# Sums of squares of queries and keys on column groups of TensorE, in plain 32-bit precision

## The chip, the cores and the metric

The kernel runs on one core of a Trainium2 chip. The metric is the device time of one execution in microseconds; of the kernel before there are three runs. All engines of the core have their own instruction stream and are kept in step by semaphores: TensorE (PE, its weight loads PEld), VectorE (DVE), ScalarE (ACT), GpSimd (POOL) and SyncE (SP), which issues the loads.

## The reference

A layer in two steps on 1024 tokens of width 256. The first is cross attention over 16 sequences of 64 tokens, 16 heads of 128, in which queries and keys are normed per head; the second is causal self attention with 16 heads and a routed gated network. Here the first matters:

```python
def rmsnorm(x, g, eps=1e-5):
    var = jnp.mean(jnp.square(x), axis=-1, keepdims=True)
    return x * jax.lax.rsqrt(var + eps) * g
q = rmsnorm((hidden_states @ Wq).reshape(B, Sq, H, D), gq)
k = rmsnorm((encoder_hidden_states @ Wk).reshape(B, Skv, H, D), gk)
scores = jnp.einsum('bqhd,bkhd->bhqk', q, k) * scale
attn = jax.nn.softmax(scores, axis=-1)
out = jnp.einsum('bhqk,bkhd->bqhd', attn, v)
return out.reshape(B, Sq, H * D) @ Wo
```

So each query and each key needs the sum of squares over its 128 channels.

## The kernel before

The tokens are cut in two halves of 512 (HT), each four tiles of 128 (NT). The stages run in the order a (cross attention) half 0 and 1, b (self attention) half 0 and 1, m (gated network) half 0 and 1. A unit of stages a and b is one head (16 a half), a unit of stage m one chunk of 128 hidden channels (25 a half). Each engine's stream is written out by hand: a function `head(u)` per engine issues, for unit u, the scores and softmax of u together with the projections of the next unit (`nxt`) and the weight splits of the one after (`after`). Beside some units stand pieces of other work (`prepare`): the norming and turning of the tokens of a later stage, named in `plan_of`. The units between run in a hardware loop of two.

Most products are made in the 32-bit form that TensorE streams at full rate (float32r) from operands that are split into a high and a low part, with three matmuls in place of one; plain float32 operands are used for the small products, and such a matmul shows as two in the trace.

In stage a, for head u, TensorE's `head` (L629) issues: the scores of u (`scores`, L567, eight 128x64 by 128x64 float32 products on alternate halves of the array's columns, so 16 instructions); the attention-value product of the head before (`attn_values`, L587); the keys and queries of the next head (`project_keys`, `project_first`, L426, three and six matmuls of 512 columns); the output product of the head before into two accumulators (`output`, L468, twelve of 256 columns); in half 0 a product of two weights (`value_out`, L533); the sums of squares of the next head's keys (`norm_k`, L553); the turn of the attention (`turn_attn`, L575); the sums of squares of the next head's queries (`norm_q`, L540).

The sums before. Queries: ScalarE writes sq_q (float32) from bank_q, and `norm_q` multiplies each tile of it, as the stationary operand, with a column of ones, one column of bank_v a tile. Keys: ScalarE squares bank_k twice, into sq_k (float32, L768) and sq_k_hi (float32r, L769), GpSimd writes the rest sq_k_lo (L1211 is the line of all its subtractions), and `norm_k` adds both with a stationary `ones_of` that puts the even sequence of a tile on partitions 0 to 63 and the odd one on 64 to 127, four matmuls of 256 columns. Then ScalarE takes the logarithm of both (`log_k` L792, `log_q` L788), GpSimd adds them (`add_logs`, L1255), ScalarE makes the inverse root (`roots`, L798), and VectorE scales the scores with it (L1025).

VectorE's `head` (L1136) after the softmax (attention written in two halves, L1043) copies the next queries (`take_q`, L1050), writes the high parts of the weights of the head after the next (`split_first` L1061, `split_second` L1073), and in half 0 the low part of the weight product (L1159). GpSimd's `head` (L1258) issues the square split, then the low parts of those weights, then `add_logs`.

Of the kernel before, what the change touches and what calls it, by code (L numbers as in the profile page):

```python
# [32 lines left out]
P = 128  # L33
# [118 lines left out]
def flamingo_layer(nc, x, ctx_t, ctx, head_a, head_b, pair_v, chunk_m, small, out, shared_units):  # L152
# [5 lines left out]
    SETUP = 8  # L158
# [28 lines left out]
    with ExitStack() as stack:  # L187
# [22 lines left out]
        ones, ones_of = sb("ones", [P, 1]), sb("ones_of", [P, SPB, P], F32R)  # L210
# [24 lines left out]
        sq_k_hi, sq_k_lo = sb("sq_k_hi", [P, HT], F32R), sb("sq_k_lo", [P, HT], F32R)  # L235
# [48 lines left out]
        A = stage_sems("a", "wq_hi wq_lo wk_hi wk_lo q_done k_done sq_q sq_k sq_k_hi sq_k_lo qt kt scores scaled max "  # L284
# [134 lines left out]
        def _(pe):  # L419
# [116 lines left out]
            def norm_q(u):  # L536

                pe.wait_ge(A["sq_q"], u.done())
                for t in range(NT):
                    last = nc.tensor.matmul(bank_v[:, D + t:D + t + 1], sq_q[:, t * P:(t + 1) * P], ones[:],  # L540
                                            start=True, stop=True)
                last.then_inc(A["ssq_done"], 1)

            def norm_k(u):

                pe.wait_ge(A["sq_k_lo"], u.done())
                if not u.very_first:
                    pe.wait_ge(A["scaled"], u.done(1))
                for s in range(SPB):
                    for part, square in enumerate((sq_k_hi, sq_k_lo)):  # L550
                        keys = square[:].rearrange("p (t s k) -> p t s k", s=SPB, k=SEQ)[:, :, s, :]
                        first, final = s + part == 0, s + part == SPB
                        last = nc.tensor.matmul(bank_s[:, NT * SEQ:2 * NT * SEQ], ones_of[:, s, :], keys,  # L553
                                                start=first, stop=final)
                last.then_inc(A["ssk_done"], 1)
# [73 lines left out]
            def head(u):  # L629
                prev, nxt = u.prev(), u.next()  # L630

                scores(u)
                if prev and prev.deferred:
                    attn_values(prev)
                if nxt.kind == "a":
                    project_keys(nxt)
                project_first(nxt)
                second_tiles = u.kind == "b" and not u.odd
                if second_tiles:
                    project_values(u, True)  # L640
                if u.kind == "a":
                    pe.wait_ge(A["ln_q"], u.done())
                if prev:
                    pe.wait_ge(stages[prev.kind]["pv_lo"], prev.done())
                held = prepare(u)
                if prev:
                    output(prev)
                if nxt.kind == "b" and not second_tiles:
                    project_keys(nxt)
                values_of_a = u.kind == "a" and u.half == 0  # L650
                if values_of_a and not held:
                    value_out(u)
                if nxt.kind == "a":
                    norm_k(nxt)
                turn_attn(u)
                if nxt.kind == "b" and second_tiles:
                    project_keys(nxt)
                for semaphore, value in held:
                    pe.wait_ge(semaphore, value)
                if values_of_a and held:  # L660
                    value_out(u)
                if nxt.kind == "a":
                    norm_q(nxt)
                if nxt.kind == "b" and not second_tiles:
                    project_values(nxt, False)
                if not u.deferred:
                    attn_values(u)
                if u.first:
                    clear_acc(u)
# [26 lines left out]
            norm_k(start)  # L696
            for kind, half in STAGES:
                run_units(pe, kind, half, chunk if kind == "m" else head)
# [3 lines left out]
        def _(act_e):  # L702
# [63 lines left out]
            def square_k(u):  # L766
                act_e.wait_ge(A["k_done"], u.done())
                nc.scalar.activation(sq_k[:], bank_k[:], ACT.Square, scale=SCALE).then_inc(A["sq_k"], 1)  # L768
                nc.scalar.activation(sq_k_hi[:], bank_k[:], ACT.Square, scale=SCALE).then_inc(A["sq_k_hi"], 1)  # L769
# [15 lines left out]
            def log_q(u):  # L785

                act_e.wait_ge(A["ssq_done"], u.done())
                nc.scalar.activation(ln_q[:], bank_v[:, D:D + NT], ACT.Ln, bias=eps5[:, 0:1]).then_inc(A["ln_q"], 1)  # L788
# [123 lines left out]
        def _(v):  # L912
# [141 lines left out]

            def split_first(u, user):
# [80 lines left out]
            def head(u):  # L1136
# [6 lines left out]
                take_q(nxt)  # L1143
                split_first(after, u)
# [55 lines left out]
            take_q(start)  # L1200
            split_first(start.next(), None)
# [6 lines left out]
        def _(pool):  # L1208
# [38 lines left out]
            def split_squares(u):  # L1247
                if u.kind == "a":
                    pool.wait_ge(A["sq_k_hi"], u.done())
                    rest(sq_k_lo[:], sq_k[:], sq_k_hi[:], A["sq_k_lo"])  # L1250

# [6 lines left out]
            def head(u):  # L1258
                nxt = u.next()
                after = nxt.next()  # L1260
                split_squares(nxt)
# [25 lines left out]
            nc.gpsimd.memset(ones_of[:].bitcast(F32), 0.0).then_inc(setup_pool, 1)  # L1287
            pool.wait_ge(setup_pool, SETUP - SPB)
            for s in range(SPB):
                nc.gpsimd.memset(ones_of[:, s, s * SEQ:(s + 1) * SEQ].bitcast(F32), 1.0).then_inc(setup_pool, 1)  # L1290
# [9 lines left out]
            split_squares(start)  # L1300
# [75 lines left out]
```

## Time and profile before

| what | value |
|---|---|
| runs | 749.43, 747.45, 749.66 us (median 749.43) |
| profiled execution, span from the first to the last instruction | 746.0 us |
| profiled execution, its own time around the span | not shown on the page |
| mean granted TensorE clock | 0.995 |
| busy: TensorE, weight loads | 724.7 us (97%), 640.1 us (86%) |
| busy: VectorE, ScalarE, GpSimd | 512.8 (69%), 370.9 (50%), 316.0 us (42%) |
| HBM | 49.3 MB by the load queue, 66 GB/s |

Times are in microseconds from the first instruction, means in nanoseconds. "Busy" of TensorE is the union of records whose ends are modelled and overlap the next start, so a share of 97% does not say that it streams all the time; the distance between the starts of matmuls says how fast it goes. A row of the timeline merges equal instructions that follow one another: its duration reaches from the first start to the last end. "Idle before" names the instruction of another engine that ended the wait.

### The profile page before, as it was taken

The numbers are of one execution on the slowest core, as the hardware profiler recorded it, in microseconds if no ns is written. First come the engines' busy times: TensorE is split into PE (matmuls) and PEld (weight loads), VectorE is DVE, ScalarE is ACT, GpSimd is POOL, SyncE is SP. The second block draws the span as 40 slices with busy tenths as digits, with TensorE's granted clock in tenths as the row PEclk, the third lists the DMA queues.
The fourth block names the chain that finished last, engine by engine and source line by source line (L and its number), as shares of the span: only waits on it lengthen the run. The fifth ranks groups of instructions, "written<-read, shape, count | busy, mean of one in ns | idle before, by whom it ended". The sixth has DMA issues, their size and how long they took to land.

```text
span 746.0 us, 15617 instructions
## 1 busy us (share of the span) xinstructions
PE 724.7 (97%) x5370; PEld 640.1 (86%) x5370; DVE 512.8 (69%) x1129; ACT 370.9 (50%) x776; POOL 316.0 (42%) x404
## 2 busy tenths in 40 slices
PE   7999999999998899999999999999999999999997
PEld 5899998888897789998888998888888888888886
DVE  4576768756576776778786787887655688655555
ACT  3667776657667533333443443334444754444442
POOL 3434343433443424333434333442555466555553
PEclk9999999999999999999999999999999999999999
DMA  8112121000100011221211221121233332333332
GB/s 277 43 44 63 42 64 54 22 25 29 32 22 22 7 45 58 86 62 58 78 57 58 89 61 57 58 65 36 70 100 85 85 85 85 88 102 85 94 95 85
DMA packets 36588, 49.88 MB, mean 67 GB/s; under 512 B 3904, under 2 KB 23744, under 8 KB 36544
## 3 DMA queue, kind: packets, MB, share of 16 engines
q1 hardware_dynamic: 36544, 49.29, 22.6%
q8 instruction: 28, 0.46, 0.3%
q14 instruction: 16, 0.13, 0.1%
HBM read 48.22 MB, written 1.05 MB: 66 GB/s over the span
## 4 chain that ended last, share of the span: by engine, by line
PE 66%; DVE 19%; ACT 5%; issue 4%; POOL 3%; DMA 2%; SPq 1%; DVEq 0%; POOLq 0%
PE acc L468 15%; PE bank_q L426 11%; PE bank_k L426 10%; PE bank_p L587 6%; PE bank_v L525 5%; PE bank_s L426 4%; PE bank_v L426 4%; PE bank_s L567 4%; PE bank_t L575 2%; PE bank_v L540 2%; DMA raw_b<-in_head_b 2%; DVE attn L1043 2%; DVE pv_lo L1015 1%; DVE qt L1050 1%; DVE sc_sub L1034 1%
## 5 line engine op out<-in xcount | busy, mean ns | idle before, releaser
L468 PE MATMUL acc<-wo_hi,pv_hi 128*128 128x256 f32 x328 | 93.4, 285 | 2.0 <-DVE pv_lo L1112 1.4
L468 PE MATMUL acc<-wo_hi,pv_lo 128*128 128x256 f32 x328 | 92.6, 282 | 0.0
L468 PE MATMUL acc<-wo_lo,pv_hi 128*128 128x256 f32 x328 | 92.0, 280 | 0.0
L1211 POOL TENSOR_TENSOR wq_lo<-raw_b,wq_hi 128x256 fp32r<-128x256 f32 x32 | 24.1, 753 | 152.3 <-DVE wq_hi L1064 152.3
L1211 POOL TENSOR_TENSOR sq_k_lo<-sq_k,sq_k_hi 128x512 fp32r<-128x512 f32 x32 | 41.2, 1288 | 79.0 <-ACT sq_k_hi L769 79.0
L426 PE MATMUL bank_q<-xt_hi,wq_hi 128*128 128x512 f32 x178 | 73.9, 415 | 0.0
L1211 POOL TENSOR_TENSOR wq_lo<-raw_m,wq_hi 128x256 fp32r<-128x256 f32 x50 | 43.4, 869 | 67.0 <-DVE wq_hi L1067 67.0
L426 PE MATMUL bank_q<-xt_hi,wq_lo 128*128 128x512 f32 x178 | 70.5, 396 | 0.0
L426 PE MATMUL bank_q<-xt_lo,wq_hi 128*128 128x512 f32 x178 | 70.5, 396 | 0.0
L1015 DVE TENSOR_TENSOR pv_lo<-bank_p,pv_hi 128x512 fp32r<-128x512 f32 x64 | 43.9, 686 | 35.8 <-ACT pv_hi L803 35.8
L468 PEld LDWEIGHTS acc<-wo_hi,pv_hi 128*128 128x128 f32 x328 | 61.7, 188 | 6.9 <-DVE pv_lo L1112 2.2
L468 PEld LDWEIGHTS acc<-wo_lo,pv_hi 128*128 128x128 f32 x328 | 61.7, 188 | 2.6
L824 ACT ACTIVATE ex<-sc_sub 128x256 f32<-128x256 f32 x64 | 26.8, 418 | 70.7 <-DVE sc_sub L1034 69.4
L468 PEld LDWEIGHTS acc<-wo_hi,pv_lo 128*128 128x128 f32 x328 | 61.8, 188 | 0.0
L815 ACT ACTIVATE pv_hi<-hh 128x512 fp32r<-128x512 f32 x50 | 31.6, 632 | 59.5 <-DVE hh L1108 59.5
L1043 DVE TENSOR_TENSOR attn<-ex,ex_inv 64x256 f32<-64x256 f32 x128 | 57.4, 448 | 4.2
L1112 DVE TENSOR_TENSOR pv_lo<-hh,pv_hi 128x512 fp32r<-128x512 f32 x50 | 36.7, 734 | 34.2 <-ACT pv_hi L815 34.2
L1101 DVE TENSOR_TENSOR gu<-gs,unit_w 128x512 f32<-128x512 f32 x44 | 32.3, 734 | 37.6 <-ACT gs L809 37.3
L803 ACT ACTIVATE pv_hi<-bank_p 128x512 fp32r<-128x512 f32 x64 | 38.2, 597 | 39.2 <-PE bank_p L587 39.1
L1211 POOL TENSOR_TENSOR wk_lo<-raw_m,wk_hi 128x256 fp32r<-128x256 f32 x50 | 40.6, 811 | 37.7 <-ACT wk_hi L869 37.7
L1211 POOL TENSOR_TENSOR wq_lo<-raw_a,wq_hi 128x256 fp32r<-128x256 f32 x32 | 23.3, 727 | 68.9 <-DVE wq_hi L1061 68.9
L1037 DVE TENSOR_REDUCE ex_sum<-ex 128x4 f32<-128x256 f32 x64 | 26.9, 420 | 31.5 <-ACT ex L824 31.5
(192 smaller groups left out, 2166.4 us busy)
## 6 DMA issues: line engine op xcount, KB each, us to landing
raw_m<-in_chunk_m SPq DMA_DIRECT2D x50, 256.0 KB, 2.7
raw_a<-in_head_a SPq DMA_DIRECT2D x48, 192.0 KB, 2.4
raw_b<-in_head_b SPq DMA_DIRECT2D x32, 256.0 KB, 2.8
raw_m<-in_chunk_m SPq DMA_DIRECT2D x50, 128.0 KB, 2.0
raw_v<-in_pair_v SPq DMA_DIRECT2D x16, 256.0 KB, 2.6
raw_b<-in_head_b SPq DMA_DIRECT2D x32, 128.0 KB, 2.0
xs<-in_x SPq DMA_DIRECT2D x8, 128.0 KB, 3.7
out<-xs SPq DMA_DIRECT2D x4, 256.0 KB, 2.3
```

Source lines behind the costliest of these rows:

```text
L426: last = nc.tensor.matmul(bank[:], w[:, cols], m(k), start=n == 0, stop=n == 3 * chunks - 1)
L468: last = nc.tensor.matmul(acc[t // 2][:, (t % 2) * D:(t % 2 + 1) * D], w[:, tok], m, start=False, stop=True, skip_group_check=True)
L525: last = nc.tensor.matmul(bank_v[:, b * PAIR:(b + 1) * PAIR], m, w[:, cols], start=n == 0, stop=n == 3 * KD - 1)
L567: last = nc.tensor.matmul(bank_s[s * SEQ:(s + 1) * SEQ, t * SEQ:(t + 1) * SEQ], qt[:, tok], kt[:, tok], start=True, stop=True)
L587: last = nc.tensor.matmul(bank_p[:, t * P:(t + 1) * P], value, attn_t[:, t * P:(t + 1) * P], start=True, stop=True)
L803: nc.scalar.activation(pv_hi[u.parity][:], bank_p[:], ACT.Copy).then_inc(stage["pv_hi"], 1)
L815: nc.scalar.activation(pv_hi[u.parity][:], hh[:], ACT.Copy).then_inc(M["hh_hi"], 1)
L1015: nc.vector.tensor_tensor(pv_lo[u.parity][:], bank_p[:], pv_hi[u.parity][:], ALU.subtract).then_inc(stage["pv_lo"], 1)
L1043: nc.vector.tensor_tensor(attn[rows, :, s * SEQ:(s + 1) * SEQ], ex[rows], ex_inv[rows].unsqueeze(2).to_broadcast([SEQ, NT, SEQ]), ALU.mult)\
L1101: nc.vector.tensor_tensor(gu[:], gs[:], weights, ALU.mult).then_inc(M["weighted"], 1)
L1112: nc.vector.tensor_tensor(pv_lo[u.parity][:], hh[:], pv_hi[u.parity][:], ALU.subtract).then_inc(M["hh_lo"], 1)
L1211: nc.gpsimd.tensor_tensor(lo, raw, hi, ALU.subtract).then_inc(signal, 1)
```

## The change

The query sums turn the operands round: a 128x32 piece of ones is stationary and sq_q streams, tile t going to partitions 32t to 32t+31 of bank_p. VectorE copies that 128x128 block (`take_rows`), TensorE transposes it into bank_q (`turn_q`), and ScalarE reads its sums from there. The key sums take sq_k alone, in float32, with 64 columns of ones stationary, one matmul for each half of the partitions. sq_k_hi, sq_k_lo and GpSimd's square split go. `norm_q` moves up to right behind `output` (where a piece is held, behind that), and the wait for the logarithm of the query sums moves up ahead of `project_first`, which overwrites bank_q.

```diff
--- before.py
+++ after.py
@@ -155,7 +155,8 @@
     C = ctx.shape[1]
     CH = chunk_m.shape[0]
     E = 16
-    SETUP = 8
+    SETUP = 6
+    GROUP = 32
     TOP = 6
     WARM_UP = 20
     HT = TOK // HALVES
@@ -207,7 +208,7 @@
         xt_hi = [sb(f"xt_hi{h}", [P, KD, HT], F32R) for h in range(HALVES)]
         xt_lo = [sb(f"xt_lo{h}", [P, KD, HT], F32R) for h in range(HALVES)]
         hn = sb("hn", [P, NT, D])
-        ones, ones_of = sb("ones", [P, 1]), sb("ones_of", [P, SPB, P], F32R)
+        ones, ones_w = sb("ones", [P, 1]), sb("ones_w", [P, SEQ])
         zeros = sb("zeros", [P, 512], F32R)
         eps5, eps6 = sb("eps5", [P, 1]), sb("eps6", [P, 1])
         tg = sb("tg", [P, 2])
@@ -232,7 +233,7 @@
         vo_hi, vo_lo = sb("vo_hi", [P, H, D], F32R), sb("vo_lo", [P, H, D], F32R)
 
         sq_q, sq_k = sb("sq_q", [P, HT]), sb("sq_k", [P, HT])
-        sq_k_hi, sq_k_lo = sb("sq_k_hi", [P, HT], F32R), sb("sq_k_lo", [P, HT], F32R)
+        rows_q = sb("rows_q", [P, P])
         qt, kt = sb("qt", [P, HT]), sb("kt", [P, HT])
         vs = sb("vs", [P, NT, PAIR])
         ln_k, ln_q = sb("ln_k", [P, NT, SEQ]), sb("ln_q", [P, NT])
@@ -281,7 +282,7 @@
 
             return {n: sem(f"{tag}_{n}") for n in names.split()}
 
-        A = stage_sems("a", "wq_hi wq_lo wk_hi wk_lo q_done k_done sq_q sq_k sq_k_hi sq_k_lo qt kt scores scaled max "
+        A = stage_sems("a", "wq_hi wq_lo wk_hi wk_lo q_done k_done sq_q sq_k rows_done rows qt kt scores scaled max "
                        "sub exp sum inv norm_lo norm_hi t_done attn_t vo_done vo_hi vo_lo ssk_done ssq_done ln_q "
                        "ln_k ln_qk r_qk pv_done pv_hi pv_lo wo_done")
 
@@ -537,21 +538,25 @@
 
                 pe.wait_ge(A["sq_q"], u.done())
                 for t in range(NT):
-                    last = nc.tensor.matmul(bank_v[:, D + t:D + t + 1], sq_q[:, t * P:(t + 1) * P], ones[:],
+                    rows = slice(t * GROUP, (t + 1) * GROUP)
+                    last = nc.tensor.matmul(bank_p[rows, 0:P], ones_w[:, 0:GROUP], sq_q[:, t * P:(t + 1) * P],
                                             start=True, stop=True)
-                last.then_inc(A["ssq_done"], 1)
+                last.then_inc(A["rows_done"], 1)
+
+            def turn_q(u):
+
+                pe.wait_ge(A["rows"], u.done())
+                nc.tensor.transpose(bank_q[:, 0:P], rows_q[:], ident).then_inc(A["ssq_done"], 1)
 
             def norm_k(u):
 
-                pe.wait_ge(A["sq_k_lo"], u.done())
+                pe.wait_ge(A["sq_k"], u.done())
                 if not u.very_first:
                     pe.wait_ge(A["scaled"], u.done(1))
                 for s in range(SPB):
-                    for part, square in enumerate((sq_k_hi, sq_k_lo)):
-                        keys = square[:].rearrange("p (t s k) -> p t s k", s=SPB, k=SEQ)[:, :, s, :]
-                        first, final = s + part == 0, s + part == SPB
-                        last = nc.tensor.matmul(bank_s[:, NT * SEQ:2 * NT * SEQ], ones_of[:, s, :], keys,
-                                                start=first, stop=final)
+                    keys = sq_k[:].rearrange("p (t s k) -> p t s k", s=SPB, k=SEQ)[:, :, s, :]
+                    last = nc.tensor.matmul(bank_s[s * SEQ:(s + 1) * SEQ, NT * SEQ:2 * NT * SEQ], ones_w[:], keys,
+                                            start=True, stop=True)
                 last.then_inc(A["ssk_done"], 1)
 
             def scores(u):
@@ -634,17 +639,19 @@
                     attn_values(prev)
                 if nxt.kind == "a":
                     project_keys(nxt)
+                if u.kind == "a":
+                    pe.wait_ge(A["ln_q"], u.done())
                 project_first(nxt)
                 second_tiles = u.kind == "b" and not u.odd
                 if second_tiles:
                     project_values(u, True)
-                if u.kind == "a":
-                    pe.wait_ge(A["ln_q"], u.done())
                 if prev:
                     pe.wait_ge(stages[prev.kind]["pv_lo"], prev.done())
                 held = prepare(u)
                 if prev:
                     output(prev)
+                if nxt.kind == "a" and not held:
+                    norm_q(nxt)
                 if nxt.kind == "b" and not second_tiles:
                     project_keys(nxt)
                 values_of_a = u.kind == "a" and u.half == 0
@@ -659,8 +666,10 @@
                     pe.wait_ge(semaphore, value)
                 if values_of_a and held:
                     value_out(u)
+                if nxt.kind == "a" and held:
+                    norm_q(nxt)
                 if nxt.kind == "a":
-                    norm_q(nxt)
+                    turn_q(nxt)
                 if nxt.kind == "b" and not second_tiles:
                     project_values(nxt, False)
                 if not u.deferred:
@@ -694,6 +703,7 @@
             project_first(start)
             norm_q(start)
             norm_k(start)
+            turn_q(start)
             for kind, half in STAGES:
                 run_units(pe, kind, half, chunk if kind == "m" else head)
 
@@ -766,7 +776,6 @@
             def square_k(u):
                 act_e.wait_ge(A["k_done"], u.done())
                 nc.scalar.activation(sq_k[:], bank_k[:], ACT.Square, scale=SCALE).then_inc(A["sq_k"], 1)
-                nc.scalar.activation(sq_k_hi[:], bank_k[:], ACT.Square, scale=SCALE).then_inc(A["sq_k_hi"], 1)
 
             def take_k(u):
                 if u.kind == "a":
@@ -785,7 +794,8 @@
             def log_q(u):
 
                 act_e.wait_ge(A["ssq_done"], u.done())
-                nc.scalar.activation(ln_q[:], bank_v[:, D:D + NT], ACT.Ln, bias=eps5[:, 0:1]).then_inc(A["ln_q"], 1)
+                sums = bank_q[:, 0:P].rearrange("p (t c) -> p t c", c=GROUP)[:, :, 0]
+                nc.scalar.activation(ln_q[:], sums, ACT.Ln, bias=eps5[:, 0:1]).then_inc(A["ln_q"], 1)
 
             def log_k(u):
                 act_e.wait_ge(A["ssk_done"], u.done())
@@ -1052,6 +1062,11 @@
                     v.wait_ge(B["q_done"], u.done())
                     nc.vector.tensor_copy(qt[:], bank_q[:]).then_inc(B["qt"], 1)
 
+            def take_rows(u):
+
+                v.wait_ge(A["rows_done"], u.done())
+                nc.vector.tensor_copy(rows_q[:], bank_p[:, 0:P]).then_inc(A["rows"], 1)
+
             def split_first(u, user):
 
                 if user:
@@ -1141,6 +1156,8 @@
                 if turning:
                     prepare_piece(*piece_at(u), u)
                 take_q(nxt)
+                if nxt.kind == "a":
+                    take_rows(nxt)
                 split_first(after, u)
                 if after.kind != "m":
                     split_second(after, u)
@@ -1198,6 +1215,7 @@
             prepare_piece("norm", ("x", 0))
             prepare_piece("turn", ("x", 0))
             take_q(start)
+            take_rows(start)
             split_first(start.next(), None)
             split_second(start.next(), None)
             for kind, half in STAGES:
@@ -1244,11 +1262,6 @@
                     pool.wait_ge(M["wd_hi"], u.done())
                     rest(wo_lo[u.parity][:], raw_m2[u.parity][:], wo_hi[u.parity][:], M["wd_lo"])
 
-            def split_squares(u):
-                if u.kind == "a":
-                    pool.wait_ge(A["sq_k_hi"], u.done())
-                    rest(sq_k_lo[:], sq_k[:], sq_k_hi[:], A["sq_k_lo"])
-
             def add_logs(u):
                 pool.wait_ge(A["ln_k"], u.done())
                 pool.wait_ge(A["ln_q"], u.done())
@@ -1258,7 +1271,6 @@
             def head(u):
                 nxt = u.next()
                 after = nxt.next()
-                split_squares(nxt)
                 split_first(after)
                 split_second(after)
                 if nxt.kind == "a":
@@ -1284,10 +1296,7 @@
             nc.gpsimd.memset(attn[:], 0.0).then_inc(setup_pool, 1)
             nc.gpsimd.memset(eps5[:], 1e-5).then_inc(setup_pool, 1)
             nc.gpsimd.memset(eps6[:], 1e-6).then_inc(setup_pool, 1)
-            nc.gpsimd.memset(ones_of[:].bitcast(F32), 0.0).then_inc(setup_pool, 1)
-            pool.wait_ge(setup_pool, SETUP - SPB)
-            for s in range(SPB):
-                nc.gpsimd.memset(ones_of[:, s, s * SEQ:(s + 1) * SEQ].bitcast(F32), 1.0).then_inc(setup_pool, 1)
+            nc.gpsimd.memset(ones_w[:], 1.0).then_inc(setup_pool, 1)
             def split_context(half):
                 pool.wait_ge(ctxt_hi_ready, half + 1)
                 toks = slice(half * HT, (half + 1) * HT)
@@ -1297,7 +1306,6 @@
             split_first(start)
             split_second(start)
             split_context(0)
-            split_squares(start)
             split_first(start.next())
             split_second(start.next())
             add_logs(start)
```

## Rows read from the trace of the kernel before

**Rows 1.** Page, part 1: busy us (share of the span) xinstructions.

```profile
PE 724.7 (97%) x5370; PEld 640.1 (86%) x5370; DVE 512.8 (69%) x1129; ACT 370.9 (50%) x776; POOL 316.0 (42%) x404
```

**Rows 2.** Timeline, a head of half 0: start us, us, engine line op out<-in xcount.

```profile
62.24 0.59 PE L533 MATMUL bank_v<-raw_a 128*128 128x256 f32 x2
...
63.03 0.28 PE L553 MATMUL bank_s<-sq_k_lo,ones_of 128*128 128x256 f32 x1
...
63.16 0.60 PE L575 MATMUL bank_t<-sm,attn 128*128 128x128 f32 x4
...
63.35 0.47 ACT L792 ACTIVATE ln_k<-bank_s,eps 128x256 f32<-128x256 f32 x1 [1.15 <-PE bank_s L553]
...
63.59 0.95 PE L540 MATMUL bank_v<-ones,sq_q 128*128 128x1 f32 x8
...
63.79 0.60 ACT L840 ACTIVATE attn_t<-bank_t 128x512 f32<-128x512 f32 x1
...
64.47 0.69 PE L567 MATMUL bank_s<-kt,qt 128*64 128x64 f32 x16
...
65.08 1.16 PE L587 MATMUL bank_p<-attn_t,ctx_sb 128*128 128x128 f32 x8
...
68.18 0.28 PE L468 MATMUL acc<-vo_hi,pv_hi 128*128 x1
...
69.60 0.59 PE L533 MATMUL bank_v<-raw_a 128*128 128x256 f32 x2
...
71.83 0.69 PE L567 MATMUL bank_s<-kt,qt 128*64 128x64 f32 x16
```

**Rows 3.** Timeline of TensorE, a head of half 1.

```profile
165.47 0.69 PE L567 MATMUL bank_s<-kt,qt 128*64 128x64 f32 x16
...
170.98 0.28 PE L553 MATMUL bank_s<-sq_k_lo,ones_of 128*128 128x256 f32 x1
171.25 0.66 PE L575 MATMUL bank_t<-sm,attn 128*128 128x128 f32 x4
...
172.63 0.28 PE L567 MATMUL bank_s<-kt,qt 128*64 128x64 f32 x2
```

**Rows 4.** Timeline of VectorE and GpSimd, the same head of half 1.

```profile
164.07 0.69 DVE L1050 COPY qt<-bank_q 128x512 f32<-128x512 f32 x1
164.80 0.29 DVE L1061 CAST wq_hi<-raw_a 128x256 fp32r<-128x256 f32 x1
...
165.17 0.73 POOL L1211 TENSOR_TENSOR wq_lo<-raw_a,wq_hi 128x256 fp32r<-128x256 f32 x1 [1.87 <-DVE wq_hi L1061]
...
166.27 0.61 POOL L1255 TENSOR_TENSOR ln_qk<-ln_k,ln_q 128x256 f32<-128x256 f32 x1
...
167.37 0.42 DVE L1025 TENSOR_TENSOR sc<-bank_s,r_qk 128x256 f32<-128x256 f32 x1 [2.14 <-ACT r_qk L798]
...
171.23 0.69 DVE L1050 COPY qt<-bank_q 128x512 f32<-128x512 f32 x1
```

**Rows 5.** Groups: attention of 30:120 us, then of 157:215; squares of the whole span.

```profile
L1043 DVE TENSOR_TENSOR attn<-ex,ex_inv 64x256 f32<-64x256 f32 x24 | 12.6, 524 | 0.8
...
L1043 DVE TENSOR_TENSOR attn<-ex,ex_inv 64x256 f32<-64x256 f32 x16 | 6.7, 420 | 0.5
...
L1211 POOL TENSOR_TENSOR sq_k_lo<-sq_k,sq_k_hi 128x512 fp32r<-128x512 f32 x32 | 41.2, 1288 | 79.0 <-ACT sq_k_hi L769 79.0
```

**Rows 6.** Group of the smallest cast of VectorE, 30:225 us.

```profile
L1073 DVE CAST wk_hi<-raw_a 128x128 fp32r<-128x128 f32 x26 | 5.7, 220 | 0.0
```

**Rows 7.** Timeline of TensorE in narrow windows around the scores of 64.47.

```profile
64.29 0.25 PE L540 MATMUL bank_v<-ones,sq_q 128*128 128x1 f32 x1
...
64.75 0.40 PE L567 MATMUL bank_s<-kt,qt 128*64 128x64 f32 x8
65.08 0.49 PE L587 MATMUL bank_p<-attn_t,ctx_sb 128*128 128x128 f32 x2
```

**Rows 8.** Tile bank_s: engine op xcount: duration ns min/median/max, first and last start, forms.

```profile
L567 PE MATMUL bank_s<-kt,qt x1024: 221/222/369, 19.8 to 517.2; 128*64 128x64 f32 x171
```

## The prediction

> **What bounds the kernel now.** The times first: three runs, median 749.43 us. The page's first part says that TensorE holds a matmul record 97% of the span [rows 1]; the ends of these records are modelled, so I read the distance between starts instead. All edits lie in stage a (32 heads out of 64, then 50 chunks), so I cut one steady head out of each half of that stage.
>
> Half 0 [rows 2]: the score matmuls (L567) start at 64.47 and again at 71.83, one head in 7.36 us. In between nothing on TensorE has a hole: twelve output matmuls of 256 columns take 69.60 - 68.18 = 1.42, 0.118 each; the value product (L533) starts at 62.24; the last of the four sums of key squares (L553) at 63.03, so it ends its slot at 63.15 and the four took 4 x 0.12 = 0.48, which leaves 62.67 - 62.24 = 0.43 for L533; the turn of the attention (L575) follows at 63.16, the query sums (L540) at 63.59, the scores at 64.47. L575 stands right at the end of the slot before it, so what it reads wasn't late. TensorE binds this half.
>
> Half 1 has no L533, so its TensorE work is 7.36 - 0.43 = 6.93. Its head takes 172.63 - 165.47 = 7.16 [rows 3]: TensorE waits, 170.98 + 0.12 = 171.10 to 171.25 in front of L575, for the attention. What makes the attention late is a ring over four engines [rows 4]: VectorE copies qt at 164.07, as soon as it has written the attention; then wq_hi at 164.80, GpSimd wq_lo at 165.17, wk_lo, the sum of logarithms at 166.27, ScalarE's root, VectorE's scaling at 167.37, the softmax, and the next qt at 171.23. From qt to qt 7.16, and each link starts when the one before it ends. So two loops matter: TensorE's list (7.36 and 6.93) and the ring. In half 0 the ring also closes in 7.36, since there the two attention products take 524 ns on average against 420 in half 1 [rows 5], 0.21 for the pair, while GpSimd's square split overlaps them. Without that it is 7.15.
>
> **The ring after.** It gains one link: take_rows stands on VectorE between qt and wq_hi. No 128x128 copy out of PSUM is in the trace. Lower bound: the 128x128 cast, 0.22 [rows 6]; upper bound: qt, four times the columns, with its distance to the next instruction, 164.80 - 164.07 = 0.73. The 128x256 read of PSUM (L1025, 0.42) and the 128x512 one (0.69) [rows 4] give (0.69 - 0.42)/256 = 1.05 ns a column, so 128 columns are 0.69 - 384 x 0.00105 = 0.29; I take 0.30. Its wait for rows_done is no cost, because norm_q now runs right behind the output product. What the edit takes from the ring is only the overlap with the square split: 0.21 in half 0, nothing in half 1. sq_k_hi on ScalarE (one instruction a head) and the split on GpSimd (32 x 1.29) [rows 5] lie beside TensorE work otherwise; their removal I cost at nothing, and at most at a gain of 0.2 a head, if ScalarE's exponential stands behind sq_k_hi on the ring. The ring becomes 7.15 + 0.30 = 7.45 in both halves. Bounds of the link 0.22 and 0.73: 7.37 to 7.88.
>
> **TensorE's list after.** Removed: the four L553 (0.48) and the eight L540. Those reach from 63.59 to 64.29 + 0.11 = 64.40 [rows 2, 7], 0.81. Together 1.29. Added: eight passes of 128 columns with a 32-wide stationary, four passes of 256 columns with a 64-wide one, and one transpose (a quarter of L575's 0.43: 0.11). The scores are the only matmuls on column groups in the trace, and they show both sides of the trade. Gain: the last eight start within 0.40 less the 0.22 of one record, 0.18, so 0.026 apart [rows 7, 8], where half of a 128-column pass (L587: eight take 1.16 - 0.28 = 0.88 from first to last start, 0.21 of it the first step, so 0.67/6 = 0.112 each) would be 0.056; two groups run at once. Cost: from the end of L540, 64.40, to the first score 0.07, and the start is slow by 0.04 (0.69 - 0.22 = 0.47 from first to last start, against 15 steps of 0.028, 0.43); at the far end the last score has ended its slot at 64.93 + 0.06 = 64.99, the next full-width matmul starts at 65.08, and from it to its follower are 0.49 - 0.28 = 0.21 instead of 0.11 [rows 7]. One excursion into column groups and back costs 0.11 + 0.20 = 0.31.
> Query sums: with two groups at once 8 x 0.112 / 2 = 0.45, plus 0.31 = 0.76. Key sums: a 256-column pass is 0.216 (half of L533), 4 x 0.216 / 2 = 0.43, plus 0.31 = 0.74. With the transpose 1.61 added, 1.29 removed: +0.32 a head. List: 7.68 in half 0, 7.25 in half 1. Bounds: four groups at once and no excursion cost, 0.22 + 0.43 + 0.11 = 0.76, i.e. -0.53; nothing at once and both excursions, 1.21 + 1.17 + 0.11 = 2.49, i.e. +1.20. I take the middle since it is the row of the scores, the nearest.
> In the trace the way out of column mode costs about 0.2 us [rows 7]. The Trainium skill says why (TensorEngine Tiling (Array Packing), Key Properties): changing the tiling mode drains the engine. By that rule the change adds two such changes back and forth where one was, and the trace agrees. Against it stands a rule of the page TensorE: Matmul & The Clock Gate (Part 3): column tiles overlap nearly fully, span about one matmul plus 4 ns a tile. By it the query sums would stream 0.23 instead of 0.45, an estimate from that page; half 0 would then be bound by the ring.
>
> **Waits that the edits add.** (a) PE waits for ln_q before project_first, since bank_q now holds the turned sums. Behind it are six projections. ln_q would end about 1.5 us after the scores start, project_first comes 2.3 after (its six matmuls of 0.233 end at 68.18): no cost, 0.3 at worst. (b) turn_q waits for rows: attention end + qt 0.72 + rows 0.32 = 1.05 behind it, and turn_q stands 0.43 behind the start of L575. Where the ring binds, TensorE idles there but nothing is added: the period is the larger of the two loops. (c) Scores wait for ln_k (0.47 [rows 2]); before, 0.88 of query sums lay between L575 and the scores, now 0.11. ln_k ends about 0.5 behind the start of L575, scores come at 0.61: no wait. But attn_t follows in ScalarE's queue (ends 64.39, where L587 starts at 65.08 [rows 2]): it would now end 1.3 behind the start of L575, where L587 wants to start at 1.23: 0.07 in half 0, hidden in half 1. I leave it in the range. (d) In the two heads whose unit turns tokens (one in each half), norm_q stands behind the turn: norm_q, rows and turn_q follow one another with nothing between, 0.3 more each, 0.6.
>
> **The sum.** Half 0: the larger of 7.45 and 7.68 against 7.36: +0.32, 15 heads, 4.8. Half 1: the larger of 7.45 and 7.25 against 7.15: +0.30, 16 heads, 4.8. Heads with a VectorE piece beside them are longer but hang on VectorE, so the copy costs them the same. Plus (d) 0.6. Prologue: two memsets fewer on GpSimd come out in the warm-up matmuls, and the first scores wait for ln_k as before: 0. Stages b and m have no edit. In all +10.2 us on the profiled execution's span of 746.0, i.e. 756.2. The page gives no time for it around the span; the median of the runs lies 3.4 above the span, and with that left as it is: 759.6; I say 759.5.
>
> **Rivals.** (1) Passes run in the order of issue: the two passes of one group can't overlap, so only neighbours do: query sums five steps of 0.112 + 0.31 = 0.87, key sums three of 0.216 + 0.31 = 0.96; list +0.65: half 0 8.01 + 0.07, half 1 7.58. 15 x 0.72 + 16 x 0.43 + 0.6 = 18: 768. For it: both passes of a score share a group. Against: the scores start in even pairs. (2) No overlap at all for these shapes: +1.20: half 0 8.56, half 1 8.13: 15 x 1.2 + 16 x 0.98 + 0.6 = 34: 784. The scores speak against it. (3) The excursions cost nothing here and four groups run at once; then only the ring binds, with the copy at 0.22: half 0 7.37, half 1 +0.22: 4 us, 753; if the ring has 0.2 of play that I don't see, it is no change, 750. (4) Faster: TensorE's list binds both halves and the ring gives way, because what GpSimd and ScalarE drop shortens it by more than the copy adds. The place is L575, the price the list's -0.53 in 15 heads of half 0: -8, 741. It decides once streams and excursions together are below the 1.29 removed and the ring below 7.36. Against it: half 1 lost 0.43 of TensorE work and gained only 0.20.
>
> **Chances.** My forecast 0.57 (its own range 756 to 763), rival 1 0.18, rival 2 0.05, rival 3 0.14 (half of it within no change), rival 4 0.06. A difference under 0.3%, 2.2 us, can't be told from none. Faster 0.06, same 0.07, slower 0.87. Range 752.5 to 769.
>
> **What would show it.** Right: the head of half 1 at about 7.45, with wq_hi 1.03 behind qt instead of 0.73, and TensorE idle before turn_q; the head of half 0 at about 7.7 with no TensorE hole; 0.1 to 0.2 at each change of column mode; the attention product at 420 ns in half 0. Wrong: a rows copy far from 0.29, starts of the new sums that are not 0.06 (queries) and 0.11 (keys) apart on average, or a wait for ln_k before the scores.

## The result: slower by 0.53%, less than half of the forecast

| kernel | median us | runs | ratio to before, 95% interval |
|---|---|---|---|
| before | 747.48 | 8 | |
| changed | 751.95 | 8 | 1.0053 [1.0034, 1.0072] |

The change costs 4.5 us. The forecast was +10.2 us, 759.5, range 752.5 to 769: the right side, less than half of the size, and 0.55 us below the range. Of the 7.5 us between 759.5 and 751.95, 2 lie in the base: the forecast stood on the 749.43 of three runs, where eight give 747.48. The other 5.6 are the change's own price.

Two words of the prediction come back below. TensorE's list is what TensorE has to work through in one head, one piece behind the other. The ring is the loop over VectorE, GpSimd and ScalarE that makes the attention of a head; a link is one instruction of it. The longer of the two sets the time of a head.

The changed kernel's page, part 1 (answers to [rows 1]): GpSimd is busy for 41 us less and ScalarE for 21, TensorE for 2.8 more.

```profile
PE 727.5 (97%) x5402; PEld 608.9 (81%) x5402; DVE 515.1 (68%) x1161; ACT 349.7 (46%) x744; POOL 274.7 (37%) x370
```

**Half 0**, the timeline of the changed kernel, one head (answers to [rows 2]):

```profile
64.28 0.28 PE L469 MATMUL acc<-vo_hi,pv_lo 128*128 x1
64.49 0.43 PE L542 MATMUL bank_p<-sq_q,ones_w 128*32 128x128 f32 x8
64.84 0.70 PE L534 MATMUL bank_v<-raw_a 128*128 128x256 f32 x2
65.47 0.65 PE L558 MATMUL bank_s<-sq_k,ones_w 128*64 128x256 f32 x4
66.06 0.66 PE L580 MATMUL bank_t<-sm,attn 128*128 128x128 f32 x4
66.17 0.47 ACT L802 ACTIVATE ln_k<-bank_s,eps 128x256 f32<-128x256 f32 x1 [1.66 <-PE bank_s L558]
66.55 0.27 PE L549 MATMUL bank_q<-sm,rows_q 128*128 128x128 f32 x1
66.79 0.69 PE L572 MATMUL bank_s<-kt,qt 128*64 128x64 f32 x16
...
74.34 0.69 PE L572 MATMUL bank_s<-kt,qt 128*64 128x64 f32 x16
```

Scores to scores 7.55, before 7.36. The eight query passes take 0.43 from the first start to the last end; one record is about 0.27 long, so all eight start within 0.16, and with the 0.11 of the last pass they stream for 0.27. Two passes of one group take 0.22 alone (0.11 each, as in the attention's turn): the four groups run at once. The output ends its slot at 64.40 and the weight product works from 64.94 (its second pass starts 0.32 behind its first instead of 0.22, so I count the 0.10 to the way out, as in [rows 7]): the query sums cost 0.55, where I had 0.76. From the end of the weight product at 65.37 to the turn of the attention (0.05 after its first start, which waits for its load) are 0.74: the key sums as forecast. Where the 0.10 and the 0.05 belong is my choice; the sum of both, 1.29, is not. The transpose is 0.11.

**Half 1**, the ring (answers to [rows 4]), timeline of VectorE and GpSimd:

```profile
182.81 0.69 DVE L1060 COPY qt<-bank_q 128x512 f32<-128x512 f32 x1
...
183.42 0.28 DVE L1068 COPY rows_q<-bank_p 128x128 f32<-128x128 f32 x1
183.73 0.29 DVE L1076 CAST wq_hi<-raw_a 128x256 fp32r<-128x256 f32 x1
...
184.10 0.72 POOL L1229 TENSOR_TENSOR wq_lo<-raw_a,wq_hi 128x256 fp32r<-128x256 f32 x1 [5.64 <-DVE wq_hi L1076]
...
190.16 0.69 DVE L1060 COPY qt<-bank_q 128x512 f32<-128x512 f32 x1
```

qt to qt 7.35, before 7.16, and even from head to head; the scores of these heads come alternately 7.03 and 7.67 apart (7.35 on average), so below a half 1 is told by its mean. The row copy lasts 0.28, as worked out, but starts 0.08 before the end of qt: from qt to wq_hi are 0.92 where 0.73 were, so the link is worth 0.19, not 0.30.

**Where VectorE was slowed.** The groups of the attention products, 30:120 us (answers to [rows 5]), then the subtraction of the maximum in the head that turns tokens, in the kernel before with the GpSimd instruction beside it, and in the changed one:

```profile
L1053 DVE TENSOR_TENSOR attn<-ex,ex_inv 64x256 f32<-64x256 f32 x24 | 10.1, 420 | 0.8
```
```profile
127.02 1.27 POOL L1211 TENSOR_TENSOR sq_k_lo<-sq_k,sq_k_hi 128x512 fp32r<-128x512 f32 x1 [2.51 <-ACT sq_k_hi L769]
127.58 0.99 DVE L1034 TENSOR_TENSOR sc_sub<-sc,sc_max 128x256 f32<-128x256 f32 x1
```
```profile
131.36 0.42 DVE L1044 TENSOR_TENSOR sc_sub<-sc,sc_max 128x256 f32<-128x256 f32 x1
```

Beside GpSimd's square split that subtraction took 0.99, without it 0.42, so 0.57 of VectorE's time is gone. The head itself, from scores to scores, fell only from 10.05 to 9.76: the query edit takes part of it again (see the key edit alone, where it is 8.91).

### The profile page after: what moved, and what is told of

It reads as the page before. It is cut to its first block, busy times and chain, and to the rows that moved or that the text cites. A ratio compares the mean times of both kernels' runs of the same rounds, so it can differ in the third digit from the quotient of the medians.

```text
span 752.2 us, 15661 instructions
## 1 busy us (share of the span) xinstructions
PE 727.5 (97%) x5402; PEld 608.9 (81%) x5402; DVE 515.1 (68%) x1161; ACT 349.7 (46%) x744; POOL 274.7 (37%) x370
## 4 chain that ended last, share of the span: by engine, by line
PE 70%; DVE 18%; ACT 4%; issue 3%; POOL 2%; DMA 2%; SPq 1%; DVEq 0%; POOLq 0%
PE acc L469 16%; PE bank_q L427 12%; PE bank_k L427 10%; PE bank_p L592 6%; PE bank_v L526 5%; PE bank_s L427 4%; PE bank_v L427 4%; PE bank_s L572 4%; PE bank_t L580 3%; PE bank_s L558 2%; DVE attn L1053 1%; DVE pv_lo L1025 1%; DMA raw_b<-in_head_b 1%; PE bank_v L534 1%; DVE sc_sub L1044 1%
## 5 line engine op out<-in xcount | busy, mean ns | idle before, releaser
L1053 DVE TENSOR_TENSOR attn<-ex,ex_inv 64x256 f32<-64x256 f32 x128 | 53.8, 420 | 4.2
L850 ACT ACTIVATE attn_t<-bank_t 128x512 f32<-128x512 f32 x64 | 38.2, 597 | 21.1 <-PE bank_t L580 18.0
```

The costliest lines, as they stand in the source:

```text
L850: nc.scalar.activation(attn_t[:], bank_t[:], ACT.Copy).then_inc(stage["attn_t"], 1)
L1053: nc.vector.tensor_tensor(attn[rows, :, s * SEQ:(s + 1) * SEQ], ex[rows], ex_inv[rows].unsqueeze(2).to_broadcast([SEQ, NT, SEQ]), ALU.mult)\
```

## Experiments

All times of heads are distances between first scores. "Steady" is the mean of 13 heads of half 0 and of 9 of half 1; the last four intervals around the end of half 0 and the last five of half 1 hold the heads with a piece beside them. Before: steady 7.36 and 7.15, sums 34.98 and 43.39. Changed: 7.55 and 7.33, 35.00 and 42.82. The expectations weigh theory A (list and ring, with the prices above) against theory B (the query rows and the moved waits are the loss, the key edit is harmless).

**The clock in these sums.** They can't be compared as they stand. In some executions TensorE runs part of one of these heads at 1.2 GHz. The same interval, the fourth of the nine, is 8.39 us before and 7.20 with the key edit alone, and it is 8.06 and 6.90 in two executions of the changed kernel. Its windows (the third number from the end is the granted clock), before, key edit alone, changed in its second profile:

```profile
149.93:158.32 8.39, 8.39 (x62) 7.68 (x62) 4.64 (x11) 4.24 (x8) 1.60 (x2) 0.83 0.08 23
```
```profile
151.57:158.77 7.20, 7.20 (x62) 6.18 (x62) 4.43 (x11) 4.26 (x8) 0.59 (x1) 1.00 0.10 28
```
```profile
151.67:158.57 6.90, 6.90 (x63) 5.53 (x63) 4.62 (x12) 3.37 (x8) 0.09 (x1) 1.00 0.09 29
```

The column probe below, in which the square split and the query sums are those of the kernel before, has 7.14 there at full clock. So 1.25 of the 34.98 before and 1.16 of the 35.00 changed are clock: 33.7 and 33.8 without them.

**Key edit alone.** The diff of the sums, on the kernel before:

```diff
-                    for part, square in enumerate((sq_k_hi, sq_k_lo)):
...
+                    last = nc.tensor.matmul(bank_s[s * SEQ:(s + 1) * SEQ, NT * SEQ:2 * NT * SEQ], ones_w[:], keys,
```

> The kernel before with the key edit alone (float32, two column groups of 64, no second square, no square split on GpSimd); query sums as before. Theory A (two loops with prices): TensorE's list gains 0.735 - 0.48 = +0.25 a head, so half 0 goes from 7.36 to 7.61; the ring gets no link and stays at 7.15, so half 1 is bound by a list of 6.93 + 0.25 = 7.18, about where it was; the heads with a VectorE piece beside them get back up to 0.5 each, because the square split no longer slows VectorE. In all +1 to +3 us. Theory B (the loss comes from the query rows and the moved waits, key edit harmless): no change or a little faster.

Measured 747.7, ratio 0.9996 [0.9982, 1.0011]. No change, where +1 to +3 us was expected. Steady heads 7.62 and 7.19, as expected; the heads with a piece gave back more than I allowed, sums 32.45 and 41.59, that is 2.5 and 1.8 us less than before. 1.25 of the 2.5 is the clock; 3.1 in all is left for the square split, 1.14, 0.95 and 0.95 of it in three of the long heads (10.05 to 8.91, 9.41 to 8.46, 9.73 to 8.78). So the key edit's price in half 0, 3.4, and its gain in the heads with pieces cancel but for the scatter of the runs. One head in the timeline of TensorE, 7.62 from scores to scores:

```profile
65.34 0.69 PE L566 MATMUL bank_s<-kt,qt 128*64 128x64 f32 x16
...
71.00 0.65 PE L552 MATMUL bank_s<-sq_k,ones_w 128*64 128x256 f32 x4
...
72.96 0.51 PE L566 MATMUL bank_s<-kt,qt 128*64 128x64 f32 x10
```

**Query edit alone.** On the changed kernel:

```diff
-                pe.wait_ge(A["sq_k"], u.done())
+                pe.wait_ge(A["sq_k_lo"], u.done())
...
+                split_squares(nxt)
                 split_first(after)
```

> The changed kernel with the key sums of before (split squares, four full-width matmuls). Theory A: the list changes by 0.55 + 0.11 + 0.06 - 0.81 = -0.09, the ring by the row copy, +0.20, and the square split keeps slowing VectorE: half 0 up to 7.5, half 1 7.35, heads with a piece 0.2 longer: +5 to +6 us on before, so slower than the whole change (+4.5) although it holds only half of its edits. Theory B: as the whole change, +4.5. A rival C (column groups for the keys are the loss): near no change.

Measured 751.57, ratio 1.0058 [1.0036, 1.0079]: as much as the whole change, not more. By their totals the two single edits come out as theory B has it; the heads decide against B, since the key edit alone makes each steady head of half 0 0.26 longer. Steady 7.41 and 7.34. So the net loss is the query edit's: the key edit pays for itself. Half 1 is the ring with its link. The heads with a piece, sums 34.10 and 43.74, are some 0.7 above those of before at full clock (33.7 and 43.39) in all. The attention products of half 0 still take 451 ns on average, against 420: 0.06 a head.

**Rows copied later on VectorE.**

```diff
                 take_q(nxt)
-                if nxt.kind == "a":
-                    take_rows(nxt)
                 split_first(after, u)
                 if after.kind != "m":
                     split_second(after, u)
+                if nxt.kind == "a":
+                    take_rows(nxt)
```

> The changed kernel, but VectorE copies the rows after the two weight casts instead of ahead of them, so the copy is off the ring. Theory A: the ring is back at 7.15, the list (7.52 and 7.09) is not: half 0 stays at 7.55, half 1 falls from 7.35 to about 7.15: 2.5 to 3 us faster than the changed kernel, +1.5 to +2 on before. Theory B: turn_q and the scores come later, so no gain, or slower.

Measured 752.05, ratio 1.0057 [1.0035, 1.0080]: no gain. Steady 7.63 and 7.31. My expectation was wrong, since there is a second ring, through TensorE. The timeline of this kernel, half 1:

```profile
170.19 0.69 DVE L1025 TENSOR_TENSOR pv_lo<-bank_p,pv_hi 128x512 fp32r<-128x512 f32 x1 [0.25 <-ACT pv_hi L813]
...
174.33 0.28 DVE L1068 COPY rows_q<-bank_p 128x128 f32<-128x128 f32 x1
...
174.67 0.14 PEld L549 LDWEIGHTS bank_q<-sm,rows_q 128*128 128x128 f32 x1 [0.33 <-DVE rows_q L1068]
...
174.93 0.69 PE L572 MATMUL bank_s<-kt,qt 128*64 128x64 f32 x16
```

TensorE now waits for the rows, the scores and all behind them come later, and so does pv_hi, for which VectorE waits 0.25 in the middle of the softmax in every second head; the copies of qt come alternately 7.20 and 7.51 apart. The copy had only changed rings.

**Rows copied by ScalarE.**

```diff
+            def take_rows(u):
+                act_e.wait_ge(A["rows_done"], u.done())
+                nc.scalar.activation(rows_q[:], bank_p[:, 0:P], ACT.Copy).then_inc(A["rows"], 1)
...
+                if nxt.kind == "a" and not turning:
+                    take_rows(nxt)
                 if nxt.kind == "a":
                     log_k(nxt)
```

> The changed kernel, but ScalarE copies the rows (ahead of the logarithm of the keys), in the place of its dropped second square; turn_q then waits for the copy of the queries too. Theory A: as the late copy on VectorE, half 1 7.15, half 0 at the list, 7.5: +1.5 to +2 us on before, and VectorE is the shorter by 0.28 a head. Theory B: no gain on the changed kernel.

Measured 748.65, ratio 1.0009 [0.9995, 1.0024]: 3.3 us of the 4.5 are gone. Steady 7.55 and 7.12: half 0 is still the list's, half 1 is back at the ring without a link. ScalarE copies beside qt:

```profile
186.67 0.28 ACT L797 ACTIVATE rows_q<-bank_p 128x128 f32<-128x128 f32 x1 [0.53 <-PE bank_p L542]
186.67 0.69 DVE L1071 COPY qt<-bank_q 128x512 f32<-128x512 f32 x1
187.39 0.29 DVE L1082 CAST wq_hi<-raw_a 128x256 fp32r<-128x256 f32 x1
```

**The two sums side by side.**

```diff
-                if nxt.kind == "a" and not held:
-                    norm_q(nxt)
...
                 if values_of_a and not held:
                     value_out(u)
+                if nxt.kind == "a" and not held:
+                    norm_q(nxt)
```

> The changed kernel with the weight product (value_out) ahead of the query sums, so that the query and key sums stand side by side in half 0 as they do in half 1. Theory A (each way into and out of column groups costs time on TensorE's list): from the end of the output product to the turn of the attention half 1 of the changed kernel takes 1.08, half 0 less its weight product 1.28; so half 0 falls by 0.20 a head to 7.35: 3 us faster than the changed kernel. Rival (the modes cost nothing, half 0 is held by a wait): half 0 stays at 7.55.

Measured 750.13, ratio 1.0020 [1.0000, 1.0039], against a before of 748.56 on that chip. Steady 7.36 and 7.31: the 0.19 of half 0, as expected.

**Both moves.**

> Both moves: rows copied by ScalarE, query and key sums side by side. Theory A: list 7.35 in half 0 and 6.9 in half 1, ring 7.15: half 0 at 7.35, half 1 at 7.12: 3 us less than with the copy on ScalarE alone (748.65), 745.6, and so 2 us faster than the kernel before. Rival: no gain from the place of the sums, 748.6.

Measured 746.27, ratio 0.9968 [0.9950, 0.9986], with both diffs above: 0.3% faster than the kernel before. Steady 7.35 and 7.12. This is the version that beats both. Its steady heads are nearly those of the kernel before (0.3 us in all), so they don't explain the gain of 2.4 us. Part of it is the clock: the mean granted clock of its 12 runs is 0.999, of the runs before 0.995, and where the whole run had 1.000 its four runs took 744.2 to 744.9 and the two of before 745.6 and 745.7, about 1.2 less. Whether the edits bring the steadier clock no run shows. The heads with a piece are 1.7 shorter than before at full clock (sums 32.96 and 42.41 against 33.7 and 43.39), but stage b is as much longer (252.4, see below), so where the rest of the gain lies stays open. Timeline of TensorE, half 0, the sums now without a full-width product between them:

```profile
70.31 0.69 PE L573 MATMUL bank_s<-kt,qt 128*64 128x64 f32 x16
75.47 0.59 PE L534 MATMUL bank_v<-raw_a 128*128 128x256 f32 x2
75.99 0.43 PE L542 MATMUL bank_p<-sq_q,ones_w 128*32 128x128 f32 x8
76.35 0.65 PE L559 MATMUL bank_s<-sq_k,ones_w 128*64 128x256 f32 x4
76.93 0.66 PE L581 MATMUL bank_t<-sm,attn 128*128 128x128 f32 x4
77.67 0.53 PE L573 MATMUL bank_s<-kt,qt 128*64 128x64 f32 x11
```

**What the way in and out costs, by itself.** Two probes on the kernel before, one execution each; the second uses `ident` and 128 partitions instead:

```diff
+                nc.tensor.matmul(bank_v[0:32, D + 16:D + 17], ones_w[:, 0:32], ones[:], start=True, stop=True)
```

> The kernel before with one additional float32 matmul of one column ahead of each weight product of half 0, on a column group of 32 (its result is not used). It streams next to nothing, so it prices the way in and out. Theory A: 0.3 a head, half 0 from 7.36 to 7.66. Rival (free): 7.4.

> Control to the probe: the same matmul at full width (stationary 128x128, result not used). Two loads of 0.112 that nothing hides: half 0 at 7.36 + 0.22 = 7.58, with no gap at either end. If the column probe is not above this one less about 0.17 (its loads are a quarter), the way in and out costs nothing.

Half 0 7.71 and 7.58, half 1 as before (7.15). So a 32-wide product of one column costs 0.35, a full-width one 0.22. The full-width loads start 0.11 apart, and two of them that nothing covers are the 0.22; the 32-wide loads start 0.026 apart, so 0.05 of the 0.35 is loads. The way in and out is 0.3. The column probe, then the full one:

```profile
65.53 0.69 PE L571 MATMUL bank_s<-kt,qt 128*64 128x64 f32 x16
70.77 0.22 PE L546 MATMUL bank_v<-ones,ones_w 128*32 128x1 f32 x2
...
73.25 0.69 PE L571 MATMUL bank_s<-kt,qt 128*64 128x64 f32 x16
```
```profile
66.03 0.69 PE L571 MATMUL bank_s<-kt,qt 128*64 128x64 f32 x16
71.17 0.28 PE L546 MATMUL bank_v<-ones,sm 128*128 128x1 f32 x2
...
73.61 0.57 PE L571 MATMUL bank_s<-kt,qt 128*64 128x64 f32 x12
```

**Query edit alone, rows by ScalarE.** The query-only kernel with the ScalarE copy above.

> The query edit alone with the rows copied by ScalarE; key sums as before (second square, square split on GpSimd, full-width matmuls). Theory A: list 7.36 - 0.09 = 7.27 in half 0, ring without a link but with the square split beside VectorE; half 0 7.25 to 7.35, half 1 7.15, heads with a piece as before: 746 to 747, 1 us faster than before. If the query copy on VectorE was not what the query edit cost, it stays near the 751.6 of the query edit alone.

Measured 748.60, ratio 1.0013 [0.9997, 1.0030]. Half 1 came out (7.14), half 0 not: 7.42, expected 7.25 to 7.35. The logarithm of the keys ends at 70.93 + 0.47 = 71.40, the scores start at 71.55, and TensorE stands idle after the transpose:

```profile
70.93 0.47 ACT L812 ACTIVATE ln_k<-bank_s,eps 128x256 f32<-128x256 f32 x1 [0.79 <-PE bank_s L563]
71.17 0.27 PE L552 MATMUL bank_q<-sm,rows_q 128*128 128x128 f32 x1
71.55 0.45 PE L577 MATMUL bank_s<-kt,qt 128*64 128x64 f32 x8
```

That is the wait for ln_k that I had ruled out: in every steady head of half 0 here the scores start 0.15 behind the end of ln_k and 0.28 behind the slot of the transpose. The changed kernel shows the same 0.15 between the end of ln_k (66.64) and the scores (66.79), so it may pay some 0.06 for it there; no run took that wait away.

**Second profiles of both kernels.**

> The kernel before, unchanged, for a second profile: how far the start (first scores at 19.75) and stage b (250.7) move from one execution to another. In stage b nothing was edited. If the 250.7 comes out near 252 here, the +1.8 of stage b between the two profiles is not the change's.

> The changed kernel, unchanged, for a second profile. Theory A: steady heads again 7.55 and 7.33; the first scores back near 19.5 (in the first profile TensorE ran its second warm-up at the low clock, which no edit causes); stage b 252 to 252.5 if it is the change's, 250.5 to 252.5 if it is chance.

The first scores came at 21.67 and 19.74, the reverse of the first pair (19.75 and 21.90). The stretch 0:16 us of before and before again, then of changed and changed again; the last three numbers are the granted clock, the DMA share and GB/s:

```profile
0.00:16.00 16.00, 11.39 (x45) 8.75 (x46) 6.84 (x22) 6.45 (x11) 5.48 (x16) 1.00 0.89 281
```
```profile
0.00:16.00 16.00, 10.78 (x37) 8.42 (x38) 6.63 (x22) 6.45 (x11) 5.47 (x16) 0.89 0.88 279
```
```profile
0.00:16.00 16.00, 11.14 (x36) 8.54 (x37) 6.75 (x22) 5.96 (x10) 3.80 (x13) 0.92 0.88 267
```
```profile
0.00:16.00 16.00, 12.19 (x44) 9.29 (x45) 6.78 (x22) 5.96 (x10) 3.80 (x13) 1.00 0.87 278
```

The two late starts are the two in which part of the warm-up ran at 1.2 GHz. The start is not the change's. Nor are the spells in the heads with a piece: the second profile of before has two (intervals of 8.50 and 8.54, clock 0.80 in both, sums 34.82 and 44.83), the second of the changed kernel none (33.50 and 42.83). Steady heads repeated to 0.01.

Stage b, from its first scores to its last: 250.7 twice before, 252.5 and 253.2 changed. Nearly all of it lies in the last six intervals (in sum, before 49.6 and 49.3, changed 51.3 and 52.0), where VectorE waits for a weight load, in the kernel before and in the changed one:

```profile
DVE wq_hi L1064 <- DMA raw_b<-in_head_b: 2.0, 4, 0.7
```
```profile
DVE wq_hi L1079 <- DMA raw_b<-in_head_b: 5.6, 9, 1.6
```

But the two probes, which hold no edit of the sums, show 252.0 and 252.4 and waits of 4.8 and 5.0 us, and the key edit alone 251.2 and 2.8. Why a load of stage b lands late when stage a is edited stays open; it is up to 2 of the 4.5 us.

## Why the forecast was too high, step by step

- **Which loops bind: right.** List of TensorE in half 0, ring over VectorE, GpSimd and ScalarE in half 1. The copy on ScalarE moved half 1 alone, the place of the sums half 0 alone. I missed the second ring (rows, scores, pv_hi, pv_lo), though it did not set the time of the change itself.
- **Query sums, +0.76: mis-sized.** They cost 0.55, since all four groups stream at once. I had priced them by the pairs that the scores show; but scores can't show more than two groups. With 0.55 the list is 7.47, with the 0.06 longer way from the transpose to the scores 7.53; measured 7.55. I had weighed the rule of the Trainium skill (TensorE: Matmul & The Clock Gate, Part 3), that column tiles overlap nearly fully. By it the stream is 0.23, an estimate; the trace has 0.16 between the first and the last start plus one pass of 0.11, 0.27, so it agrees to 0.04.
- **The excursion, 0.31: right**, twice: 0.35 in the probe with some 0.05 of its own loads, and 0.19 back where one return is saved. Half 1 had the two sums side by side already, so its list was 0.2 too high; the ring hid that. The Trainium skill (TensorEngine Tiling (Array Packing), Key Properties) says that changing the tiling mode drains the engine; the 0.3 of the probe agrees.
- **Key sums +0.74, transpose 0.11: right.**
- **The row copy's link, 0.30: mis-sized.** 0.19; its end was right, its overlap with qt was not in the sum.
- **Heads with a piece, +0.30 each and +0.3 for two: a term left out.** "They hang on VectorE, so the copy costs them the same" left out that the square split slowed VectorE there too. I took that contention back only where the steady head of half 0 showed it. At full clock the nine intervals fell by about 0.5 in all, where I had about +3.3. The key edit alone gives about 3 back, and the query edit on top of it adds 2.5: the price of the copy was nearly right, the return was missing. (On average of two profiles of each kernel the two sums fell by 0.65 and 1.3; 1.4 of these 1.9 are spells at 1.2 GHz, three of them in the profiles of before and one in those of the changed kernel.)
- **Removed squares at nothing: wrong** for the same reason. This is the step that failed most: about 3 us come back where the prediction had nothing. With them and the two sizes as measured (0.13 and 0.12 less in 13 and 9 steady heads, 2.8) the sum of 10.2 becomes 4.4. That this meets the measured 4.5 so closely is partly luck, since what stage b adds is not in it.
- **Wait (c), none: not quite.** The scores stand 0.15 behind ln_k, as in the run where TensorE waits for it; in the changed kernel that is at most 0.06 a head.
- **Rival 3 had the time, 4 us and 753, but not for its reason.** Four groups do run at once, as it says, but the way in and out costs 0.3 and the list still binds half 0. That its figure is nearer than mine is luck.
- **Stage b at nothing: not settled** (above). **Prologue 0: right.**

In numbers, stage a rose by 1.7 on average (246.3 and 247.1 to 249.0 and 247.7): steady heads 13 x 0.19 + 9 x 0.18 = +4.1, the first interval -0.5, heads with pieces -1.9. The first interval ran at a clock of 0.79 and 0.77 before and at full clock in the changed kernel, so that -0.5 and 1.4 of the 1.9 go with the clock of these profiles; at full clock stage a is some 3.6 longer. Stage b adds 2.1, stage m takes 0.4. The spans of the profiled executions differ by 3.5, the medians of eight runs by 4.5.

Of the signs set beforehand, these came: the row copy at 0.28, the attention product at 420 ns, 0.1 to 0.2 at each change of column mode. These did not: 1.03 from qt to wq_hi (0.92), 7.45 and 7.7 for the heads (7.35 and 7.55). The sign of being wrong that showed is the distance of the query sums' starts, 0.02 on average instead of 0.06; a wait for ln_k may have been there too, for 0.06 at most.

## What to carry to other kernels

Price column groups as stream plus about 0.3 us for each way in and out, and set them next to each other; two passes on each of four groups took little more than two passes on one. When an instruction is added to an engine, follow every ring that it can lengthen, and give it to the engine that has just lost work. When GpSimd work goes, look for VectorE instructions that are longer beside it, above all in the heads where VectorE sets the end. Before two sums of intervals are compared, look at the granted clock of each interval.

## What the runs showed of the hardware

- A 128x256 VectorE subtraction took 0.99 us beside a GpSimd subtraction and 0.42 alone; in two other heads with a piece 1.08 and 1.12.
- Four column groups of 32 start 7 ns apart, and the second pass of a group 0.13 behind its first: eight passes of 128 columns in 0.27 us, where two alone take 0.22.
- A switch of groups from 32 to 64 columns was not free either (0.1 from the end of the last query pass to the first key pass), but cheaper than a return to full width between them by 0.2 us.
- The start of the kernel moved by 2 us with the clock that the warm-up was granted (0.89 and 0.92 against 1.00 in the first 16 us).
- In three of the four profiles of the two kernels a head beside a piece took 8.06 to 8.54 us at a mean granted clock of 0.80 to 0.84; the same heads took 6.90 to 7.20 at 1.00 in other executions.
